# Second expert bias: from a table in on-chip memory picked by a register, instead of gate transposes and bias matmuls

## The reference, cut to what matters

```
# layer 0: 8 experts, width 1024, the best one of each row (top 1)
for e in range(8):
    h = gelu(x_flat @ w1[e] + b1[e]);  y = h @ w2[e] + b2[e]
    out = out + where(expert_idx == e, expert_w, 0)[:, None] * y
# layer 2: 8 experts, width 512, the best two of each row (top 2), gates normalized to sum 1
out = einsum('besh,ehd->besd', gelu(x W1 + b1), W2) + b2[None, :, None, :]
y   = einsum('bse,besd->bsd', gates, out)
```

## Time and profile before

| | |
|---|---|
| time, median of 3 runs | 1867.71 us |
| profiled execution, first to last instruction (span) | 1836.7 us |
| median minus span (start and end outside the instructions) | 31.0 us |
| share of the chain that ended last: TensorE / VectorE / ScalarE | 69% / 15% / 6% |
| block loop of `e0`, first up matmul to last eviction | about 293 to 477 us |
| block loop of `e2` | about 1493 to 1664 us |

### The profile page before, as it was taken

How to read it: one execution, slowest core, us unless ns; L and a number is a source line. 1 busy time by engine, 2 the same in 40 slices (tenths; PEclk the granted TensorE clock), 3 DMA queues, 4 the chain that set the end, 5 groups by cost and what they waited for, 6 DMA issues and landing times.

```text
span 1836.7 us, 27973 instructions
## 1 busy us (share of the span) xinstructions
PE 1603.0 (87%) x9998; PEld 1210.8 (66%) x9998; DVE 1070.4 (58%) x3023; ACT 906.0 (49%) x2034; POOL 379.8 (21%) x480
## 2 busy tenths in 40 slices
PE   6999959999679999999858799999998779995566
PEld 5677638889557666676535567777665468894444
DVE  7767752222456676666567665555555535325887
ACT  4888821222146666666549355555554102233366
POOL 1000014111232333323240100000001332223734
PEclk9999989999789999999979899999999889997878
DMA  9000028888400000000000200000000438893001
GB/s 342 2 1 1 2 92 325 292 290 288 143 7 6 7 7 7 7 1 1 1 1 1 81 12 7 7 7 7 1 1 12 135 132 264 300 354 120 0 12 35
DMA packets 61625, 151.99 MB, mean 83 GB/s; under 512 B 9216, under 2 KB 39696, under 8 KB 55248
## 3 DMA queue, kind: packets, MB, share of 16 engines
q1 hardware_dynamic: 54096, 133.65, 22.1%
q0 software_dynamic: 5280, 14.47, 2.1%
q10 hardware_dynamic: 2112, 2.10, 0.4%
HBM read 133.63 MB, written 24.75 MB: 86 GB/s over the span
## 4 chain that ended last, share of the span: by engine, by line
PE 69%; DVE 15%; ACT 6%; POOL 4%; issue 4%; DMA 1%; POOLq 1%; SPq 0%; DVEq 0%; ACTq 0%
PE bank L1036 8%; PE bank L979 8%; PE bank L1459 8%; PE bank L1513 7%; PE bank L1526 6%; PE bank L1500 5%; PE bank L1463 5%; PE bank L1443 3%; PE bank L679 3%; POOL sorted_h L1224 2%; PE bank L695 2%; PE bank L1865 2%; PE bank L710 1%; ACT p1f L1581 1%; PE bank L616 1%
## 5 line engine op out<-in xcount | busy, mean ns | idle before, releaser
L1710 DVE TENSOR_REDUCE small<-bank 128x1 f32<-128x512 f32 x128 | 82.5, 686 | 108.8 <-PE bank L1513 108.8
L1055 ACT ACTIVATE e2a<-bank,WB 128x128 f32<-128x128 f32 x156 | 44.5, 368 | 178.6 <-PE bank L1036 178.6
L1706 DVE CUSTOM_DVE_ANT_0 p1f<-bank,p1f 128x512 f32<-128x512 f32 x128 | 83.2, 687 | 81.0 <-PE bank L1513 81.0
L1584 ACT ACTIVATE p2f<-bank,small 128x512 f32<-128x512 f32 x128 | 86.8, 683 | 86.2 <-DVE small L1710 86.2
L751 ACT ACTIVATE l<-l,small 128x256 f32<-128x256 f32 x256 | 108.9, 502 | 32.6 <-DVE small L817 32.2
L1581 ACT ACTIVATE p1f<-p1f,small 128x512 f32<-128x512 f32 x128 | 91.2, 713 | 67.5 <-DVE small L1706 67.2
L400 POOL TENSOR_SCALAR rs<-mv 128x4 f32<-128x4 f32 x16 | 3.6, 226 | 566.8 <-DVEq L230 551.1
L817 DVE CUSTOM_DVE_ANT_0 l<-bank,small 128x256 f32<-128x256 f32 x256 | 90.8, 420 | 13.4 <-PE bank L695 12.5
L1459 PE MATMUL bank<-WA,HT 128*128 128x256 f32 x384 | 93.4, 387 | 5.0 <-DVE p1f L1651 5.0
L1595 ACT ACTIVATE p2f<-bank 128x512 f32<-128x512 f32 x128 | 75.1, 598 | 40.6 <-PE bank L1500 39.1
L1055 ACT ACTIVATE e0a<-bank,WB 128x128 f32<-128x128 f32 x128 | 36.5, 367 | 106.2 <-PE bank L1036 106.2
(11 more groups left out here) (401 smaller groups left out, 3939.1 us busy)
## 6 DMA issues: line engine op xcount, KB each, us to landing
WB<-in_L2pack SPq DMA_DIRECT2D x39, 514.0 KB, 5.3
WB<-in_L2pack SPq DMA_DIRECT2D x39, 512.0 KB, 5.5
WB<-in_L0pack SPq DMA_DIRECT2D x16, 1028.0 KB, 6.4
WB<-in_L0pack SPq DMA_DIRECT2D x16, 1024.0 KB, 7.3
e0a<-in_L0pack SPq DMA_DIRECT2D x7, 1028.0 KB, 7.1
e0a<-in_L0pack SPq DMA_DIRECT2D x7, 1024.0 KB, 6.8
sorted_h<-in_blank SPq DMA_DIRECT2D x6, 1032.0 KB, 16.2
e2a<-sorted_h SPq DMA_DIRECT2D x39, 129.0 KB, 5.3
```

Source lines behind the costliest of these rows:

```text
L1584: ins = a.e.activation(P, k.bank(x), ACT.Exp, bias=self.mx[:, m:m + 1], accum_out=self.sm[:, m:m + 1])
```

## The change

The second bias is added to each block's rows as they leave PSUM. All rows of a block have the same expert, so one row of the bias table serves the block. The table (8 x 256 floats) is written by one DMA to all 128 partitions (1 MB) into `HT[:, 0, :]`, which is free during the blocks. At step `i` VectorE reads the block's expert number into a register, and the eviction becomes an addition of PSUM and the table's row at that register. It is done for every block, 23 and 39. The gate tile `G`, its two last VectorE operations in `worth`, the transposes, their copies, the bias matmuls and the additions to `X` go. The old DMA of the 8 KB table at the head of `sp` goes; the new one stands in `load_x`, ahead of the load of block 4 in `e0` and of block 2 in `e2`.

```diff
@@ __init__
-        self.L, self.G, self.E = (r(128, t=16, e=8) for _ in range(3))
+        self.L, self.E = (r(128, t=16, e=8) for _ in range(2))
-        self.b2 = r(256)
+        self.yb = k.HT[:, 0, :].rearrange("p (e n) -> p e n", e=8)
-        self.GT = [r(128) for _ in range(3)]
@@ pe
-        t.wait_ge(self.a_b2, 1)
-        t.wait_ge(self.routing, self.GATED)
@@ down_pe
-        if self.biased(i) is not None:
-            t.e.matmul(y[:, 256:512], self.GT[i % 3][0:8, :], self.b2[0:8, :], start=True, stop=True)
@@ turn_pe
-        t.wait_ge(self.routing, self.GATED)
-        if self.biased(i) is not None:
-            t.e.transpose(T[0:8, 256:384], self.G[:, self.biased(i), :], k.ident[:, :])
@@ worth
-            v.chain(e.tensor_tensor(S[:, 0, :, :], S[:, 0, :, :], S[:, 1, :, :], ALU.add))
-            e.tensor_tensor(G, S[:, 0, :, :], bc(d), ALU.mult).then_inc(self.routing.sem, 1)
-        else:
-            e.tensor_copy(G, S[:, 0, :, :]).then_inc(self.routing.sem, 1)
@@ dv
         for i in range(nt):
             if i + 2 < nt:
                 self.turn_dv(v, i + 2)
+            x = v.e.value_load(self.ex[0:1, i:i + 1], min_val=0, max_val=7)
+            v.wait_ge(self.a_b2, 1)
             v.wait_ge(self.dn, i + 1)
             v.wait_ge(self.ay[i % 3], i // 3)
-            if self.biased(i) is not None:
-                k.residual(v, self.biased(i), k.bank(4 + i % 2)[:, 256:512], None)
-            v.e.tensor_copy(self.ys[i % 3], k.bank(4 + i % 2)[:, 0:256]).then_inc(self.yc.sem, 1)
+            v.e.tensor_tensor(self.ys[i % 3].rearrange("p (o n) -> p o n", o=1), k.bank(4 + i % 2)[:, 0:256].rearrange("p (o n) -> p o n", o=1),
+                              self.yb[:, bass.ds(x, 1), :], ALU.add).then_inc(self.yc.sem, 1)
@@ turn_dv
-        if self.biased(i) is not None:
-            v.e.tensor_copy(self.GT[i % 3][0:8, :], k.bank(6 + i % 2)[0:8, 256:384])
@@ load_x
+        if i == (4 if self.two else 2):
+            s.wait_ge(self.counted, 1)
+            s.wait_ge(self.xt_d, 1)
+            s.e.dma_start(self.yb.rearrange("p e n -> p (e n)"), self.b2d.rearrange("(o e) n -> o (e n)", o=1).to_broadcast([128, 2048])).then_inc(self.a_b2.sem, 16)
         s.wait_ge(self.xt_t, i - 2)
         s.wait_ge(self.xt_d, i - 2)
         s.e.dma_start(self.xs[i % 3], self.h[i * 128:(i + 1) * 128, :]).then_inc(self.ax[i % 3].sem, 16)
@@ sp
-        s.e.dma_start(self.b2[0:8, :], self.b2d).then_inc(self.a_b2.sem, 16)
```

More of the change, by code:

```diff
@@ L847 @@
 class Experts:
-    SHIFTED, SELECTED, PLACED, KNOWN, GATED = 1, 2, 3, 4, 5
+    SHIFTED, SELECTED, PLACED, KNOWN = 1, 2, 3, 4
     def __init__(self, k, tag, heir, ff, topk, nt, temp, bias, nwb):
@@ L890, in __init__ @@
         self.cleared = (k.setup.z0, 3) if tag == "e0" else (k.setup.z2, 5)
-        self.a_b2 = k.dma("b2", 1)
         late = 3 if topk == 1 else 0
@@ L895, in __init__ @@
         self.a2 = [k.dma(f"gather{4 + i}", len(range(i, nt, nwb))) for i in range(nwb)]
+        self.a_b2 = k.dma("b2", 1)
         self.sc = k.dma("scatter", n // 2), k.dma("ey0", n // 2)
@@ L908, in __init__ @@
             self.seated, self.place_of = f("p_cxn", 4), r(4, i=2, n=2)
-        self.routing = f("e_routing", 5)
+        self.routing = f("e_routing", 4)
         self.xt_t, self.xt_d = f("e_xt_t", nt), f("e_xt_d", nt)
@@ L981, in down_pe @@
         ins.then_inc(self.dn.sem, 1)
-    def biased(self, i):
-        return i - 2 if 2 <= i < 18 else None
     def logits_pe(self, t, g):
@@ L1085, in worth @@
     def worth(self, v):
-        e, G, E, M, S = v.e, self.G, self.E, self.M, self.S
+        e, E, M, S = v.e, self.E, self.M, self.S
         topk, d, gv, bc = self.topk, self.d, self.gv, self.over
```

## The result

| | before | after |
|---|---|---|
| median of 4 runs, us | 1869.26 (1862.19 to 1872.19) | 1834.48 (1830.44 to 1839.10) |
| span of the profiled execution, us | 1836.7 | 1832.1 |
| its time, us | not given | 1833.89 |

The ratio is 0.9827 [0.9805, 0.9848]. The forecast was 1837.7 us (1831 to 1847) and faster with a chance of 0.93.

A forecast was written before the change was run, and what follows sets the result against it. The prediction took never-idle TensorE to bound the blocks. Gains of 30.7 us less 0.45 for register loads and 0.3 for the table gave 30.0: span 1836.7 to 1806.7, plus 31.0 makes 1837.7 us, range 1831 to 1847.

The forecast's parts named there:

- The main term: Blocks 2 to 17 of `e0` and `e2`: 0.93 us less TensorE time in each of 2 x 16, 29.8 us.
- The ends: Corrections outside the steady loop: 0.4 us at turn(2) and turn(3) of `e0`, 0.1 and 0.4 in `e2`.
- step 3 of `e2`: TensorE waits for the weight sum; VectorE's path there shrinks from 3.13 to 2.77 us, 0.4 us more gain.
- up(3): In `e2`, after the mask reduction: the copy's 0.20 us counts and the transpose's 0.11 doesn't, 0.1 us more gain.
- The 0.15 on step 0 of `e2`: Cost of the register operation behind the wait, uncovered because that eviction leads into the mask reduction TensorE waits for.
- The register load: New on VectorE at each of 62 steps: 0.44 us, plus 0.15 behind the wait; mostly hidden, costing 0.45 us in all.
- the tight place of 3.70 in 3.73 us: Step 2 of `e2`: eviction, 2.20 us weight sum, row copies and register load on VectorE just fit in one block.
- rival 2: DMA takes TensorE's place as the bound in `e0`: all of `e0`'s gain lost, 1852 us; chance 0.06.
- rival 3: The table lands late at the head of the stages: 6.5 us back, 1844 us; chance 0.07.
- The 0.7 us and the absorption: Table in `e0` 0.7 us late for step 0's eviction, partly absorbed ahead of the next row copy; 0.3 us taken.
- Rival 5: Dear register loads make VectorE the bound of `e2`; gain eaten at 3.2 us per load, up to 1913 us; chance 0.03.
- The wrong step: Adding the 31.0 us between span and median to the predicted span of 1806.7 us, giving 1837.7 us.

The follow-up runs named there:

- half of the change: The kernel before with the change made in `e2` only, `e0` keeping transposes and bias matmuls: 1827.36 us, ratio 0.9905.
- the matmul alone: The kernel before without the bias matmuls and the additions to `X`, gate transposes and their copies kept: 1816.12 us, ratio 0.9855.
- Before again: The kernel before, unchanged, run for a second profile: 1842.82 us, ratio 0.9995, span 1845.2.
- After a third time: The changed kernel, unchanged, run once more on another chip: 1810.08 us, ratio 0.9821, span 1817.4.
- the fixed row: The changed kernel without the register load, each block adding row 0 of the table: 1812.58 us, ratio 0.9842.
- nine loads: The changed kernel with 9 register loads per step on VectorE instead of 1: 1919.87 us, ratio 1.0419.
- Four loads: The changed kernel with 4 register loads per step on VectorE instead of 1: 1822.78 us, ratio 0.9884.

## Why the prediction was right, and where it was wrong

**The main term** was 2 x 16 x 0.93 = 29.8 us, read from blocks with and without the work in one and the same profile. It held: the loops are 30.4 us shorter (30.0 forecast, 15.2 in each stage), half of the change gives 16.0, and the matmul alone 26.4, with 32 x 0.81 = 25.9 by the earlier trace rows.

**The ends.** In `e0` TensorE's two waits for row copies at turn(2) and turn(3) went from 0.85 to 0.67 us each, 0.36 together where 0.4 was forecast. At step 3 of `e2` the interval went from 6.60 to 5.49, 0.93 + 0.18 instead of 0.93 + 0.36: that term was twice too large. Three timelines of TensorE at the place show why. Before again, with transpose and bias matmul:

```profile
1530.21 0.27 PE L1017 MATMUL bank<-ident,e2a 128*8 128x128 f32 x1
1531.76 0.61 PE L2334 MATMUL bank<-small,onesf 128*128 128x1 f32 x4 [1.28 <-DVE small L2351]
```

With the transpose alone:

```profile
1512.59 0.27 PE L1015 MATMUL bank<-ident,e2a 128*8 128x128 f32 x1
1513.68 0.61 PE L2330 MATMUL bank<-small,onesf 128*128 128x1 f32 x4 [0.81 <-DVE small L2347]
```

After a third time:

```profile
1516.07 0.58 PE L2320 MATMUL bank<-small,onesf 128*128 128x1 f32 x4 [1.13 <-DVE small L2337]
```

Without the addition to `X` the wait falls from 1.28 to 0.81; in after, without the transpose right ahead of the wait and with the register operation, it is 1.13 again. The transpose's 0.11 was hidden there, and I had counted it once in the 0.93 and not taken it out, as I did at up(3). The rest is the path over VectorE: from the start of the up ahead of the wait to the weight sum's matmul it went from 3.33 to 3.07 us, 0.26 and not 0.36. The 0.15 on step 0 of `e2` was seen as 0.1.

**The register load** was 0.52 us instead of 0.44, and cost nothing by itself. The sum that put it behind the row copies had the order wrong: the loads run beside VectorE's data operations, so the tight place of 3.70 in 3.73 us wasn't tight. At the tight place of after a third time the load starts at 1511.48, ahead of the row copies at 1512.17. What remained is the operation behind the wait.

**DMA (rival 2).** At 7.24 us per block the rate rose from 279 to 328 GB/s and the share from 0.86 to 0.93; 315 and 0.97 had been worked out, and TensorE stayed busy. In `e2`, 0.31 us of idle time in the stretch of 59 us above are all; they stand ahead of one transpose of rows.

**The table (rival 3)** came in time in the first two profiles of after and was 1.0 us late in the third, without a loss for TensorE. The 0.7 us and the absorption were the right mechanism, and the 0.3 were too much there; with the fixed row, 2.5 us late, it cost TensorE 0.8.

**Rival 5** did not come. The run with nine loads shows that VectorE's queue can become the bound, but not by the rival's sum: that had 1.06 + C per block, with the neighbours' pieces on top, and the run has C + 0.7, with the pieces hidden. With 5.3 us for nine loads the rival's formula gives 37 x (5.3 - 2.67) + 4.4 + 6.6 = 108 us, the loop of `e2` 91. By the pace of 0.61 us, an estimate for this kernel: plain blocks grow from six loads a step on, and the gain is eaten between six and seven, at C of about 4 us, not 3.2. Four loads, at 0.9884, and nine, at 1.0419, lie on either side of it. That the expectation's 85 us came near is luck: 1.0 for data operations and 0.52 a load add up to nearly the step that a load every 0.61 us gives.

**The wrong step** is the last one. "With the 31.0 us between span and median" took the difference of 1867.7 and 1836.7 as something around the span. It isn't: after's profiled execution took 1833.89 us with a span of 1832.1, 1.8 us around it, and before again 1847.06 with 1845.2. If the same 1.8 us lay around the first profile of before, that execution took 1838.5 us, 24 less than the fastest timed one of the first comparison and within the 1838.2 to 1848.6 of the three later chips; on which chip it ran is not on record. The predicted 1837.7 came near 1834.48 because only a difference was laid on the median. The predicted span of 1806.7 is 25 us under the 1832.1 of after's profile: 15.5 of that is what this profile has outside the loops over after a third time, the rest mostly the short profile of before.

**Left open:** why TensorE stood still for 21 us and VectorE for 14.7 in the first profile of after, and why the same program takes 1869 us in one comparison and 1843 on three chips. The two may be one thing, but no profile of before from the slow comparison is there to show it. The 34.8 us of the first comparison, against 25.3 and 32.5 us in the other two, are one gain of about 30 us in three noisy measurements as far as the loops show it; where the rest of each lies outside the loops is not settled.

## To carry to other kernels

- Where a loop has iterations with and without a piece of work, the difference of their periods is its price, with all that it does to its neighbours. Here it gave 0.93 us where the two dropped instructions alone have 0.11 + 0.62.
- A small matmul is not always a cheap one. One with 8 rows in the middle of a full-rate stream cost more here than one with 128; the addition at the eviction cost nothing, as VectorE had room for it.
- Compare stretches, not spans, and lay a worked-out difference on the median of the same chip. One span can hold 20 us of standstill that the next doesn't have.

## What was not expected of the hardware

- A float32 matmul with 8 rows of weights and a 128x256 result takes 0.62 us and makes the 16 behind it 0.19 us longer; with 128 rows it is 0.43 and nothing.
- A register load on VectorE is 0.30 us at the least, with its two companions 0.52 laid end to end, and nine in a row follow each other every 0.61 us. They run beside VectorE's data operations: one started 0.20 us after an eviction of 0.42.
- With nine loads TensorE's granted clock in `e2` fell from 0.97 to 0.89 and the same matmuls were busy 28 us longer, without lengthening the loop, which VectorE's queue set.
- A 1 MB transfer that spreads 8 KB over 128 partitions landed in 4.3 and 6.0 us in the first profile of after; a piece of weights of that size takes 6.4. Over all runs the table took 4.3 to 7.7.
